# The flag of an exact-path branch summed on TensorE instead of GpSimd, the last projections issued ahead of the branch, and one normalised tile moved later on ScalarE

## The chip, the cores and the metric

The kernel runs on one core of one Trainium2 chip. The time is device microseconds of one execution; the kernel before had a median of 961.63 us over three executions (959.44, 961.63 and 963.8). The profiled execution took 960.48 us by the same clock, and its trace spans 958.4 us from the first to the last instruction.

## The reference

The input x has 2 x 2048 rows of 1024 numbers in float32, here 4096 tokens. What is computed, cut to what matters:

```python
xn = layernorm(x)                              # along the 1024
f = rfft(xn); corr = irfft(f * conj(f))        # autocorrelation of each token
weights, delay = top_k(corr, 6)
p = softmax(weights)
s = sum_k p[k] * roll(xn, -delay[k])
gate = silu(lin(xn, w1q, a1, b1)); up = lin(xn, w3q, a3, b3)
g = silu(lin(gate * up, w2q, a2, b2))          # lin: tiled quarter weight + 0.5 * low-rank part
out = x + s * g
```

Where the autocorrelation at lag 0 stands far above all others, the softmax puts its whole weight on lag 0 and s is xn itself. The kernel proves that for each token by a bound, and has a general path for a group in which a token fails it.

## The kernel before, in words

The 4096 tokens go through in eight groups (i = 0 to 7) of four tiles (q = 0 to 3) of 128 tokens. Each engine has a program of its own, written out in order, and semaphores tie them together. The hidden width is worked through as 22 row blocks of 128 ("pairs", p = 0 to 21; p = 21, LAST, has 64 rows).

**Up stage of group i.** For each p, TensorE makes gate and up products in three rotating pairs of banks (`up`, L1066, with the low-rank part in `lora`, L1083). ScalarE takes silu of the gate (`gate`), VectorE multiplies (`product`, L725, into `h`) and adds four pairs into a chunk (`add_chunk`, L737). Every four pairs TensorE projects `h` on a2 into the bank `zb` (`z2`, L1142). In the same stage the next group is made ready, tile by tile: VectorE's `stats(i + 1, q)` at p = 1, 7, 13, 19; GpSimd's `spread` (L439 to L444, the scale and shift of the normalisation); ScalarE's `normalise` at p = 2, 8, 14, 20 (`xn`); GpSimd's `differences` and `sums` (`ab`, `hl`, which SP's queue transposes into `ft` and `xt`); VectorE's `project` (L680, four per tile; those of tile 3 are `last_projections`).

**The flag.** At p = 5, 9, 11, 15 TensorE computes a part of the power spectrum and the lags from it in the bank `mb` (`odd_power`, `lags`), and VectorE's `lag_gap` takes maxima from it. At p = 16 `lag_gap` writes `rest` (L715): for each of 128 partitions, how many of its four tokens fail the bound. `rest_done` is signalled, and GpSimd adds `rest` over the partitions (L498, `partition_all_reduce`) as the first thing of its turn q = 3, ahead of `spread(i + 1, 3)`; in group 0 five subtractions `w2_low` (L478, 128x1024 each) stand between the two.

**Down stage of group i.** `down` multiplies the folded chunks `hf` by w2 into four token tiles: TensorE's order is chunk 0 of tile 0, `z2` of pairs 16 to 19, chunks 1 and 2, `z2` of pairs 20 and 21 (it waits for `product` of p = 21), chunks 3 and 4, chunks 0 to 4 of tile 1, the tail chunk of both tiles (L1169 ends a tile), tile 2, then `z_across(i + 1)` (four transposes of `zs`, L1128) and tile 3. Meanwhile VectorE and ScalarE finish the tail chunk (`tail_sums`, `folded_low`, in group 0 also `w2_tail`) and `z2_stack`, whose end (`z2_read`) the tail chunk waits for. Then VectorE tests the flag (L1031), loads it into a register (L1033) and branches. In both branches it runs `last_projections(i + 1)` and then, in the one that is taken here, `multiply` and `add_input` for each tile (L859, L864), with `z_split` (L690 to L698, writes `zs`) after tile 0.

ScalarE runs its program in order too: `normalise(i + 1, 3)` at p = 20 stands ahead of `gate(i, 21)`.

Of the kernel before, what the change touches and what calls it, by code (L numbers as in the profile page):

```python
# [8 lines left out]
ACT = mybir.ActivationFunctionType  # L9
ALU = mybir.AluOpType  # L10
AX_X = mybir.AxisListType.X
RADD = bass.bass_isa.ReduceOp.add

P = 128
L = 1024
# [75 lines left out]
def build(nc, d):  # L91
# [3 lines left out]
    with ExitStack() as ctx:  # L95
# [9 lines left out]
        def sem(name):  # L105
            return ctx.enter_context(nc.semaphore(name))
# [65 lines left out]
        zp = [sb(f"zp{k}", [P, 4, 4], BF16) for k in range(3)]  # L172
        rm = sb("rm", [P, 4], F32)
        gp = sb("gp", [P, 4], F32)
        rest = sb("rest", [P, 1], F32)
        rest_all = sb("rest_all", [P, 1], F32)
        some = sb("some", [P, 1], I32)
        raw_a2 = sb("raw_a2", [P, NP_, 2], F32)
        v8 = sb("v8", [P, 8], F32)
# [85 lines left out]
        diff_done, ab_done, sum_done, hl_done = sem("diff_done"), sem("ab_done"), sem("sum_done"), sem("hl_done")  # L265
        z_done, zs_done, zt_ready, zst_done = sem("z_done"), sem("zs_done"), sem("zt_ready"), sem("zst_done")
        c_ready, sq_done, i_ready, gap_done = sem("c_ready"), sem("sq_done"), sem("i_ready"), sem("gap_done")
        rest_done, rall_done = sem("rest_done"), sem("rall_done")
        g_ready, u_ready, sil_done, mult_done = sem("g_ready"), sem("u_ready"), sem("sil_done"), sem("mult_done")
        acc_done, hfh_done, hfl_done = sem("acc_done"), sem("hfh_done"), sem("hfl_done")  # L270
        shift_done, half_done, hft_done, b2h_done = sem("shift_done"), sem("half_done"), sem("hft_done"), sem("b2h_done")
# [11 lines left out]
        def at_group(i, per, n):  # L283
            return i * per + n
# [1 line left out]

        STATS_AT, NORM_AT = (1, 7, 13, 19), (2, 8, 14, 20)
        Z_AT = {3 + 6 * q + r: (q, r) for q in range(3) for r in range(4)}
        C_AT, I_AT = (5, 9), (11, 15)


        def front_buf(i, q):
# [139 lines left out]
        @block.gpsimd  # L432
        def _(pool):
            tt, cp = nc.gpsimd.tensor_tensor, nc.gpsimd.tensor_copy

            def spread(i, q):
                n = i * 4 + q
                pool.wait_ge(stats_done, n + 1)
                tt(ve[:, q:q + 1], mv[:, q, 1:2], three[:, 0:1], ALU.add).then_inc(dev_done, 1)  # L439
                tt(nm[:, q:q + 1], mv[:, q, 0:1], three[:, 2:3], ALU.mult)  # L440
                pool.wait_ge(dev_done, 3 * n + 1)
                tt(rs[:, q:q + 1], ve[:, q:q + 1], three[:, 1:2], ALU.pow).then_inc(dev_done, 1)
                pool.wait_ge(dev_done, 3 * n + 2)
                tt(nm[:, q:q + 1], nm[:, q:q + 1], rs[:, q:q + 1], ALU.mult).then_inc(dev_done, 1)  # L444

            def differences(i, q):
                n, x = i * 4 + q, normal_buf(i, q)
                pool.wait_ge(normed, n + 1)
                if i == 0:
                    pool.wait_ge(hl_done, 2)  # L450
                    if q:
                        pool.wait_ge(ab_done, 3 * n)
                tt(yh[:], x[:, 0:HALF], x[:, HALF:L], ALU.subtract).then_inc(diff_done, 1)
                if n:
                    pool.wait_ge(ft_loaded, 16 * n)
                pool.wait_ge(diff_done, n + 1)
                tt(ab[:, 1:DQ], yh[:, 1:DQ], yh[:, HALF - 1:DQ:-1], ALU.subtract).then_inc(ab_done, 1)
                tt(ab[:, DQ + 1:HALF], yh[:, 1:DQ], yh[:, HALF - 1:DQ:-1], ALU.add).then_inc(ab_done, 1)
                cp(ab[:, 0:DQ + 1:DQ], yh[:, 0:DQ + 1:DQ]).then_inc(ab_done, 1)

            def sums(i, q):
                n, x = i * 4 + q, normal_buf(i, q)
                pool.wait_ge(normed, n + 1)
                if i:
                    pool.wait_ge(ab_done, 3 * n + 3)
                tt(yh[:], x[:, 0:HALF], x[:, HALF:L], ALU.add).then_inc(sum_done, 1)
                pool.wait_ge(sum_done, at_sum(i, q, 1))
                tt(xq[:], yh[:, 0:DQ], yh[:, DQ:HALF], ALU.add).then_inc(sum_done, 1)
                if i and q == 0:
                    pool.wait_ge(xt_loaded, 16 * 4 * i)  # L470
                pool.wait_ge(sum_done, at_sum(i, q, 2))
                cp(hl[:, q, 0:DQ], xq[:]).then_inc(sum_done, 1)
                pool.wait_ge(sum_done, at_sum(i, q, 3))
                tt(hl[:, q, DQ:HALF], xq[:], hl[:, q, 0:DQ], ALU.subtract).then_inc(hl_done, 1)

            def w2_low(n):
                pool.wait_ge(w2h_done, n + 1)
                tt(w2_l[:, n, :], raw_w2[:, n, :], w2_h[:, n, :].bitcast(F32), ALU.subtract).then_inc(w2l_done, 1)  # L478

            for n, value in enumerate((EPS, -0.5, -1.0)):  # L480
                nc.gpsimd.memset(three[:, n:n + 1], value).then_inc(zeroed, 1)
            nc.gpsimd.memset(ones[:], 1.0).then_inc(zeroed, 1)
            pool.wait_ge(zeroed, 4)
            for q in range(4):
                spread(0, q)
            sums(0, 0)
            sums(0, 1)
            nc.gpsimd.memset(zs[:], 0.0).then_inc(zeroed, 1)
            for q in range(4):
                differences(0, q)  # L490
            pool.wait_ge(c_loaded, 16 * 3)
            for u in range(3):
                cp(a2st[:, :, 2 * u:2 * u + 2], raw_a2[:]).then_inc(a2_done, 1)
            for i in range(NG):
                for q in range(4):
                    if q == 3:
                        pool.wait_ge(rest_done, i + 1)
                        nc.gpsimd.partition_all_reduce(rest_all[:], rest[:], P, RADD).then_inc(rall_done, 1)  # L498
                        for n in range(HN if i == 0 else 0):
                            w2_low(n)  # L500
                    if i + 1 < NG:
                        spread(i + 1, q)
                        differences(i + 1, q)
                        sums(i + 1, q)
# [3 lines left out]
        def _(act):  # L508
# [114 lines left out]
            for i in range(NG):  # L623
                last = i + 1 == NG
                for p in range(NP_):
                    gate(i, p)
                    if i == 0 and p in HIGH_AT:
                        w_high(HIGH_AT[p])
                    if i == 0 and p in LOW_AT and LOW_AT[p][1] in (0, 2):
                        b_high(LOW_AT[p][0], LOW_AT[p][1] // 2)  # L630
                    if i == 0 and p in W2_AT:
                        w2_high(W2_AT[p])
                    if p in C_AT:
                        square(i, C_AT.index(p))
                    if not last and p in NORM_AT:
                        normalise(i + 1, NORM_AT.index(p))
                    if p % 4 == 1 and p > 1:
                        folded_high(i, p // 4 - 1)
                    if i == 0 and p == LAST:
                        b2_high()  # L640
                tail_shifts(i)
                folded_high(i, HN)
                z2_copies(i)
                for q in range(4):
                    if not last and q == 3:
                        z_copy(i + 1)
                    down(i, q)
# [3 lines left out]
        def _(dve):  # L651
# [31 lines left out]
            def last_projections(i):  # L683
                for r in range(4):
                    project(i, 3, r)
# [311 lines left out]
            nc.vector.memset(hf_l[64:P, HN, :].bitcast(F32), 0.0)  # L997
            w_tops(2, 6)
            w_scale(2, 6)
            dve.wait_ge(zeroed, 5)  # L1000
            for i in range(NG):
                last = i + 1 == NG
                current(i)
# [23 lines left out]
                if i == 0:  # L1027
                    w2_tail()
                z2_stack(i)
                dve.wait_ge(rall_done, i + 1)  # L1030
                ts(some[:], rest_all[:], 0.0, None, ALU.is_gt)  # L1031
                drain()
                flag = dve.value_load(some[0:1, 0:1])  # L1033
                with dve.If(flag > 0):
                    if not last:
                        last_projections(i + 1)
                        z_split()
                    for q in range(4):
                        general(i, q)
                with dve.Else():  # L1040
                    if not last:
                        last_projections(i + 1)
                    for q in range(4):
                        multiply(i, q)
                        add_input(i, q)
                        if not last and q == 0:
                            z_split()
# [3 lines left out]
        def _(pe):  # L1051
# [60 lines left out]
            def lags(i, k):  # L1112
# [7 lines left out]
                        o = mm(mb[:, DQ * j:DQ * j + DQ], sq[:, c, t], inv[:, 0, :], start=c == 0, stop=c == 1)  # L1120
                o.then_inc(i_ready, 1)

            def z_across(i):
                pe.wait_ge(zs_done, i)
                if i:
                    pe.wait_ge(gap_done, at_group(i - 1, 2, 2))
                for q in range(4):
                    o = nc.tensor.transpose(mb[:, q * P:(q + 1) * P], zs[:, q, :], ident[:])  # L1128
                o.then_inc(zt_ready, 1)
# [52 lines left out]
            for q in range(4):  # L1182
# [3 lines left out]
                for k in range(8):  # L1186
                    o = nc.tensor.transpose(x_banks[k][:, q * P:(q + 1) * P],
                                            normal_buf(0, q)[:, k * P:(k + 1) * P], ident[:])
                    if q == 3:
                        o.then_inc(x_ready, 1)  # L1190
            pe.wait_ge(zeroed, 4)

            def w_tops(first, count):
                pe.wait_ge(wsum_done, first + count)
# [17 lines left out]
            for i in range(NG):  # L1212
                last = i + 1 == NG
                pe.wait_ge(xt_loaded, 16 * 4 * (i + 1))
                for p in range(NP_):
# [8 lines left out]
                        odd_power(i, C_AT.index(p))  # L1224
                    if p in I_AT:
                        lags(i, I_AT.index(p))
                down(i, 0, range(0, 1))
                z2(i, ZB - 2)
                down(i, 0, range(1, 3))
# [55 lines left out]
```

## Time and profile before

| | |
|---|---|
| median of 3 executions | 961.63 us |
| profiled execution, its span | 960.48 us, 958.4 us |
| TensorE busy (matmul) | 868.9 us, 91% of the span |
| VectorE busy | 640.9 us, 67% |
| ScalarE busy | 298.6 us, 31% |
| GpSimd busy | 301.3 us, 31% |
| mean granted clock of TensorE | 0.949 of full speed |

In the rows, PE is TensorE (PEld its weight loads), DVE VectorE, ACT ScalarE, POOL GpSimd, SP the engine that issues the transfers. A row of a timeline is: start, duration (both us), engine, line, operation, out<-in, shape and count; in brackets how long the engine had been idle before it, and what it had waited for. Where several instructions are merged in a row, its duration is from the first to the last. "issue" is idle time for which the profile shows no wait. A row of stretches is: from:to, its length, then the busy time (and count of instructions) of PE, PEld, DVE, ACT and POOL, the granted clock of TensorE as a share of full speed, the busy share of the transfer engines, and GB/s.

### The profile page before, as it was taken

The page shows a single profiled execution, that of the slowest core. Times are in us where ns is not written, and L with a number is a line of the kernel's source. Part 1 is how long each engine was busy: PE and PEld are TensorE (multiplying, and loading weights), DVE is VectorE, ACT ScalarE, POOL GpSimd, SP SyncE. Part 2 cuts the span into 40 slices and gives each one's busy share as a digit, 9 for nine tenths or more (in the row PEclk, how much of TensorE's full clock was granted, in tenths as well). Part 3 has the DMA queues.
Part 4 walks back from the last instruction along what each step waited for, and adds up shares of the span by engine and source line. Part 5 has one row for each costly group of instructions (what it writes and reads, how often), then busy time and mean ns, then how long its engine had stood idle before and what let it go on. Part 6 is the DMA issues. An engine that isn't in the chain of part 4 may idle for free.

```text
span 958.4 us, 11140 instructions
## 1 busy us (share of the span) xinstructions
PE 868.9 (91%) x4034; PEld 444.6 (46%) x4034; DVE 640.9 (67%) x1007; ACT 298.6 (31%) x441; POOL 301.3 (31%) x401
## 2 busy tenths in 40 slices
PE   3868857899899997999979998999979998999997
PEld 3323325644365434843446343844447443653465
DVE  7578834777675795578846786667846776653444
ACT  4653504133222333133232332223322331323221
POOL 6444443034321443034430453133430343300000
PEclk9789977999989997999989999999979999899999
DMA  9735102321034101321124110431023210140003
GB/s 313 202 114 146 28 0 50 111 88 34 28 82 167 34 28 44 116 89 34 28 51 160 38 36 26 124 124 34 28 50 110 89 34 7 43 161 1 1 1 132
DMA packets 53719, 71.53 MB, mean 75 GB/s; under 512 B 37152, under 2 KB 39424, under 8 KB 53392
## 3 DMA queue, kind: packets, MB, share of 16 engines
q1 hardware_dynamic: 53648, 70.69, 23.8%
q8 instruction: 31, 0.51, 0.2%
q14 instruction: 40, 0.33, 0.1%
HBM read 45.51 MB, written 16.78 MB: 65 GB/s over the span
## 4 chain that ended last, share of the span: by engine, by line
PE 58%; DVE 15%; issue 11%; DVEq 7%; SPq 3%; ACT 3%; POOL 3%; DMA 0%; ACTq 0%; POOLq 0%
PE g L1066 14%; PE u L1066 13%; PE zb L1142 4%; PE g L1166 4%; PE u L1166 4%; DVEq L741 4%; DVE junk L680 4%; DVE h L725 4%; PE u L1173 3%; PE g L1173 3%; PE g L1175 3%; PE u L1175 3%; PE g L1083 2%; ACT sil L510 2%; DVE acc L737 1%
## 5 line engine op out<-in xcount | busy, mean ns | idle before, releaser
L1066 PE MATMUL g<-xt,w_h 128*128 128x512 f16 x672 | 203.3, 384 | 10.1 <-DVE w_l L911 5.5
L510 ACT ACTIVATE sil<-g,winv 128x512 f32<-128x512 f32 (+1 forms) x176 | 120.1, 683 | 268.6 <-PE g L1083 224.7
L1066 PE MATMUL u<-xt,w_h 128*128 128x512 f16 x672 | 202.0, 383 | 0.0
L725 DVE SCALAR_TENSOR_TENSOR h<-u,winv,sil 128x512 f32<-128x512 f32 x168 | 125.7, 748 | 97.8 <-ACT sil L510 83.0
L680 DVE CUSTOM_DVE_ANT_0 junk<-xn,abc 128x1024 bf16<-128x1024 f32 x112 | 155.5, 1388 | 32.2 <-issue 28.6
L439 POOL TENSOR_TENSOR ve<-mv,three 128x1 f32<-128x1 f32 x32 | 6.8, 211 | 389.6 <-DVE mv L663 339.4
L1066 PE MATMUL g<-xt,w_l 128*128 128x512 f16 x336 | 128.7, 383 | 0.0
L1066 PE MATMUL u<-xt,w_l 128*128 128x512 f16 x336 | 128.1, 381 | 0.0
L1066 PEld LDWEIGHTS u<-xt,w_h 128*128 128x128 f16 x672 | 66.3, 99 | 81.0 <-issue 3.0
L1066 PEld LDWEIGHTS g<-xt,w_h 128*128 128x128 f16 x672 | 57.2, 98 | 97.7 <-issue 35.9
L1142 PE MATMUL zb<-h,a2st 128*6 128x512 f32 (+1 forms) x352 | 70.2, 639 | 35.5 <-DVE h L725 35.5
L1166 PE MATMUL g<-w_h,hf_h 128*128 128x512 f32 x192 | 83.0, 432 | 9.9 <-POOL w_l L478 9.9
L859 DVE SCALAR_TENSOR_TENSOR ob<-xr,c_mean,gg 128x1024 f32<-128x1024 f32 x32 | 41.0, 1282 | 64.8 <-ACT gg L510 64.0
L1166 PE MATMUL u<-w_h,hf_h 128*128 128x512 f32 x192 | 79.0, 412 | 0.0
L510 ACT ACTIVATE gg<-g 128x512 f32<-128x512 f32 x32 | 19.2, 599 | 172.3 <-PE g L1169 119.0
L510 ACT ACTIVATE xn<-xf,nm,rs 128x1024 f32<-128x1024 f32 x29 | 35.9, 1239 | 102.7 <-POOL nm L444 102.7
L1173 PE MATMUL u<-w_l,hf_h 128*128 128x512 f32 x160 | 66.2, 414 | 0.0
L1173 PE MATMUL g<-w_l,hf_h 128*128 128x512 f32 x160 | 66.1, 413 | 0.0
L1175 PE MATMUL u<-w_h,hf_l 128*128 128x512 f32 x160 | 66.0, 412 | 0.0
L1175 PE MATMUL g<-w_h,hf_l 128*128 128x512 f32 x160 | 65.9, 412 | 0.0
L737 DVE TENSOR_TENSOR acc<-acc,h 128x512 f32<-128x512 f32 x80 | 64.0, 799 | 0.0
L1166 PEld LDWEIGHTS g<-w_h,hf_h 128*128 128x128 f32 x192 | 38.5, 201 | 39.5 <-issue 30.1
(163 smaller groups left out, 1184.7 us busy)
## 6 DMA issues: line engine op xcount, KB each, us to landing
xr<-in_x SPq DMA_DIRECT2D x34, 512.0 KB, 4.7
out_x<-ob SPq DMA_DIRECT2D x32, 512.0 KB, 2.9
xf<-in_x SPq DMA_DIRECT2D x30, 512.0 KB, 3.5
raw_w<-in_w2t SPq DMA_DIRECT2D x1, 2560.0 KB
raw_w<-in_w1t SPq DMA_DIRECT2D x3, 768.0 KB, 7.9
raw_w<-in_w3t SPq DMA_DIRECT2D x3, 768.0 KB, 9.5
abc<-in_a SPq DMA_DIRECT2D x1, 2048.0 KB, 14.0
xt<-hl SPq DMA_TRANSPOSE x32, 3.4
```

The costliest lines, as they stand in the source:

```text
L510: return nc.scalar.activation(out, in_, f, **kw)
L680: nc.vector.tensor_tensor_reduce(junk[:], normal_buf(i, q)[:], abc[:, r, :], 1.0, 0.0, ALU.mult, ALU.add, zt[:, q, r:r + 1]).then_inc(z_do ...
L725: stt(out=h[0:n, p % NH, :], in0=up, scalar=winv[0:n, 2 * (p // 6) + 1:2 * (p // 6) + 2], in1=sil[0:n, p % 2, :], op0=ALU.mult, op1=ALU.mu ...
L737: o = tt(acc[0:rows, b, :], a, h[0:rows, p % NH, :], ALU.add)
L741: drain()
L859: stt(out=o[:], in0=x[:], scalar=c_mean[:, q:q + 1], in1=gg[:], op0=ALU.subtract, op1=ALU.mult)
L1066: o = mm(bank[:], a, x, start=opens and t == 0, stop=closes and t == len(terms) - 1)
L1083: o = mm((gb, ub)[s % 2][k % 3][:], bst[32 * s:32 * s + 32, p // 2, :], zst[32 * s:32 * s + 32, :], start=s >= 2, stop=s < 2)
L1142: o = mm(zb[c:c + 6, :], a2st[0:rows, p, :], h[0:rows, p % NH, :], start=n == 0, stop=p + 4 >= NP_)
L1166: mm(bank[:], hf_h[:, n, t], w2_h[:, n, c:c + 512], start=n == 0, stop=False)
L1173: mm(bank[:], hf_h[:, n, t], w2_l[:, n, c:c + 512], start=False, stop=False)
L1175: mm(bank[:], hf_l[:, n, t], w2_h[:, n, c:c + 512], start=False, stop=False)
```

## The change

The sum of `rest` over the partitions goes from GpSimd to TensorE: `rest` becomes bfloat16, and one matmul of a 128x128 block of ones (`ones_h`) with it (`flag_sum`, one column, into the first column of `mb`) stands in TensorE's program behind `up(i, 18)`. VectorE's test reads `mb` instead of `rest_all`, and signals `flag_read`, for which `z_across` now waits before it overwrites `mb`. `last_projections(i + 1)` moves from both branches to ahead of the test. On ScalarE, `normalise(1, 3)`, in group 0 alone, moves from p = 20 to behind `z2_copies(0)`.

```diff
-        rest = sb("rest", [P, 1], F32)
-        rest_all = sb("rest_all", [P, 1], F32)
+        rest = sb("rest", [P, 1], BF16)
+        ones_h = sb("ones_h", [P, P], BF16)
...
-        C_AT, I_AT = (5, 9), (11, 15)
+        C_AT, I_AT, FLAG_AT = (5, 9), (11, 15), 18
...
             nc.gpsimd.memset(ones[:], 1.0).then_inc(zeroed, 1)
-            pool.wait_ge(zeroed, 4)
+            nc.gpsimd.memset(ones_h[:], 1.0).then_inc(zeroed, 1)
+            pool.wait_ge(zeroed, 5)
...
                     if q == 3:
-                        pool.wait_ge(rest_done, i + 1)
-                        nc.gpsimd.partition_all_reduce(rest_all[:], rest[:], P, RADD).then_inc(rall_done, 1)
                         for n in range(HN if i == 0 else 0):
                             w2_low(n)
...
-                    if not last and p in NORM_AT:
+                    if not last and p in NORM_AT[:3 if i == 0 else 4]:
                         normalise(i + 1, NORM_AT.index(p))
...
                 z2_copies(i)
+                if i == 0:
+                    normalise(1, 3)
...
                 z2_stack(i)
+                if not last:
+                    last_projections(i + 1)
                 dve.wait_ge(rall_done, i + 1)
-                ts(some[:], rest_all[:], 0.0, None, ALU.is_gt)
+                ts(some[:], mb[:, 0:1], 0.0, None, ALU.is_gt).then_inc(flag_read, 1)
                 drain()
                 flag = dve.value_load(some[0:1, 0:1])
                 with dve.If(flag > 0):
                     if not last:
-                        last_projections(i + 1)
                         z_split()
                     for q in range(4):
                         general(i, q)
                 with dve.Else():
-                    if not last:
-                        last_projections(i + 1)
                     for q in range(4):
...
+            def flag_sum(i):
+                pe.wait_ge(rest_done, i + 1)
+                mm(mb[:, 0:1], ones_h[:], rest[:], start=True, stop=True).then_inc(rall_done, 1)
+
             def z_across(i):
                 pe.wait_ge(zs_done, i)
-                if i:
-                    pe.wait_ge(gap_done, at_group(i - 1, 2, 2))
+                pe.wait_ge(flag_read, i)
...
                     if p in I_AT:
                         lags(i, I_AT.index(p))
+                    if p == FLAG_AT:
+                        flag_sum(i)
```

## Rows read from the trace of the kernel before

**Rows 1.** Waits of TensorE, 187 to 960 us: engine, line, releaser, us, times, longest.

```profile
PE zb L1142 <- DVE h L725: 30.4, 6, 5.6
```

**Rows 2.** Busy time in stretches: one up stage, six down stages (summed), the last one.

```profile
187.40:254.10 66.70, 66.70 (x347) 27.02 (x347) 54.51 (x84) 22.22 (x32) 27.97 (x37) 1.00 0.17 54
259.48:296.96 37.48, 32.91 (x127) 23.61 (x127) 21.43 (x34) 10.35 (x17) 8.86 (x12) 0.91 0.34 103
...
811.36:849.89 38.53, 32.91 (x126) 23.62 (x126) 21.43 (x34) 10.34 (x17) 8.85 (x12) 0.91 0.27 86
sum 230.18, PE 199.82 PEld 143.46 DVE 128.74 ACT 62.05 POOL 53.12; mean PE 33.30 PEld 23.91 DVE 21.46 ACT 10.34 POOL 8.85
921.87:951.41 29.54, 29.54 (x123) 22.29 (x122) 9.98 (x10) 5.20 (x10) 0.00 (x0) 1.00 0.25 90
```

**Rows 3.** Timelines of VectorE and GpSimd around the reduction of group 1.

```profile
246.42 0.15 DVE L715 TENSOR_SCALAR rest<-gp 128x1 f32<-128x1 f32 x1
246.13 0.67 POOL L474 TENSOR_TENSOR hl<-xq,hl 128x256 f16<-128x256 f32 x1
252.98 0.40 POOL L498 PARTITION_ALL_REDUCE rest_all<-rest  x1 [6.18 <-issue]
260.21 0.18 POOL L439 TENSOR_TENSOR ve<-mv,three 128x1 f32<-128x1 f32 x1 [6.83 <-issue]
```

**Rows 4.** Timelines of the other engines, from group 1's last statistics to TensorE.

```profile
254.42 0.21 DVE L663 BATCH_NORM_AGGREGATE mv<-bn 128x2 f32<-128x12 f32 x1
261.40 1.24 ACT L510 ACTIVATE xn<-xf,nm,rs 128x1024 f32<-128x1024 f32 x1 [7.97 <-POOL nm L444]
263.24 0.75 DVE L725 SCALAR_TENSOR_TENSOR h<-g,winv,sil 64x512 f32<-64x512 f32 x1 [7.35 <-ACT sil L510]
264.05 3.67 PE L1142 MATMUL zb<-h,a2st 128*6 128x512 f32 x4 [4.57 <-DVE h L725]
```

**Rows 5.** Timelines of VectorE and TensorE, from the flag to the transposes, groups 1 and 3.

```profile
272.86 0.15 DVE L1031 TENSOR_SCALAR some<-rest_all 128x1 int32<-128x1 f32 x1
276.82 1.23 DVE L680 CUSTOM_DVE_ANT_0 junk<-xn,abc 128x1024 bf16<-128x1024 f32 x1 [3.80 <-issue]
285.75 0.71 DVE L698 CAST zs<-zp 128x64 f32<-128x64 bf16 x6
288.58 0.60 PE L1128 MATMUL mb<-ident,zs 128*128 128x128 f32 x4
...
499.39 1.23 DVE L680 CUSTOM_DVE_ANT_0 junk<-xn,abc 128x1024 bf16<-128x1024 f32 x1 [4.69 <-issue]
508.32 0.70 DVE L698 CAST zs<-zp 128x64 f32<-128x64 bf16 x6
```

**Rows 6.** Timelines of group 0: VectorE's flag input, GpSimd, TensorE, VectorE.

```profile
120.40 0.15 DVE L715 TENSOR_SCALAR rest<-gp 128x1 f32<-128x1 f32 x1
133.31 11.63 POOL L478 TENSOR_TENSOR w_l<-raw_w,w_h 128x1024 fp32r<-128x1024 f32 x5 [7.01 <-issue]
147.94 0.75 DVE L725 SCALAR_TENSOR_TENSOR h<-g,winv,sil 64x512 f32<-64x512 f32 x1 [18.06 <-ACT sil L510]
177.45 0.66 PE L1128 MATMUL mb<-ident,zs 128*128 128x128 f32 x4 [2.81 <-DVE zs L698]
187.43 0.61 PE L1066 MATMUL g<-xt,w_h 128*128 128x512 f16 x2
```

**Rows 7.** Timelines of GpSimd and VectorE, one collision; the 0.68 us row undisturbed.

```profile
222.96 1.27 POOL L466 TENSOR_TENSOR yh<-xn 128x512 f32<-128x512 f32 x1
223.03 1.75 DVE L737 TENSOR_TENSOR acc<-h 128x512 f32<-128x512 f32 x1
227.83 0.68 DVE L737 TENSOR_TENSOR acc<-acc,h 128x512 f32<-128x512 f32 x1
```

**Rows 8.** TensorE at p = 19, where `flag_sum` is put, and `rest`: group 3.

```profile
467.38 0.39 PE L1083 MATMUL g<-zst,bst 32*128 32x512 bf16 x1
467.72 0.15 DVE L715 TENSOR_SCALAR rest<-gp 128x1 f32<-128x1 f32 x1
```

More of the change, by code:

```diff
@@ L11 @@
 AX_X = mybir.AxisListType.X
-RADD = bass.bass_isa.ReduceOp.add
 P = 128
@@ L267, in build @@
         c_ready, sq_done, i_ready, gap_done = sem("c_ready"), sem("sq_done"), sem("i_ready"), sem("gap_done")
-        rest_done, rall_done = sem("rest_done"), sem("rall_done")
+        rest_done, rall_done, flag_read = sem("rest_done"), sem("rall_done"), sem("flag_read")
         g_ready, u_ready, sil_done, mult_done = sem("g_ready"), sem("u_ready"), sem("sil_done"), sem("mult_done")
@@ L999, in _ @@
             w_scale(2, 6)
-            dve.wait_ge(zeroed, 5)
+            dve.wait_ge(zeroed, 6)
             for i in range(NG):
@@ L1190, in _ @@
                         o.then_inc(x_ready, 1)
-            pe.wait_ge(zeroed, 4)
+            pe.wait_ge(zeroed, 5)
             def w_tops(first, count):
```

## The prediction, made before the changed kernel was seen

> **What bounds the kernel now.** The page's busy shares come first: TensorE has 91% of the span, so the question is where its other 9% lies. The waits of TensorE from group 1 on have one entry, 30.4 us in six times: the last `z2` of a group waits for `product` of p = 21 [rows 1]. The stretches show the rest. In an up stage TensorE is busy for all of its 66.70 us at full clock [rows 2]. The six down stages of groups 1 to 6, each from the moment when that wait begins to the first matmul of the next group, take 230.18 us together [rows 2]; that of group 7, which has no such wait and keeps the full clock, takes 29.54 us [rows 2]. The granted clock of the six is 0.91 or so, that is, a part of each ran at 1.2 GHz instead of 2.4: TensorE had idled for 4.57 us before, and its first four matmuls afterwards take 3.67 us [rows 4]. So the wait costs its own length and then a slow stretch.
>
> Why is `product` late? It waits for the gate's silu, which stands behind `normalise(i + 1, 3)` on ScalarE, which waits for the scale from GpSimd [rows 4]. The statistics are there at 254.42 + 0.21 = 254.63, but GpSimd takes them up at 260.21, because the reduction is in its way: `rest` is there at 246.57, GpSimd is free at 246.80, and yet the 0.40 us reduction starts after 6.18 us of idling and is followed by 6.83 us more [rows 3]. The reduction takes 13.4 us of GpSimd, and 5.5 us of that end on the path.
>
> **The change, part by part.** *The reduction leaves GpSimd.* `spread(i + 1, 3)` then follows the statistics as elsewhere, about 0.08 us behind: 254.71 instead of 260.21, 5.50 us earlier. By the same reading it is 5.5 to 5.9 us in groups 2 to 6. `product` of p = 21 follows, 263.24 - 5.50 = 257.74, and is read 0.81 us after its start [rows 4], at 258.55. TensorE gets there at 264.05 - 4.57 = 259.48 [rows 4]. The wait is gone, with 0.9 us to spare (0.2 in the tightest, group 6), and with it what took the clock down. The down stage should then be group 7's 29.54 us plus the transposes of `zs`, which group 7 lacks, 0.44 us at full clock from the start of one to the next matmul (my estimate from their 0.60 us row [rows 5]): 29.98. Six of them are 179.9 us, so 230.2 - 179.9 = 50.3 us are to be had.
>
> *What is late next.* The transposes wait for `zs`. VectorE's chain (tail chunk, `z2_stack`, projections, flag, tile 0, split) has no idle time that waits for TensorE in group 1, so it moves by the same 5.50 us: `zs` is written at 285.75 + 0.71 - 5.50 = 280.96 [rows 5]. TensorE moves by more: it gets there at 288.6 to 288.7 now [rows 5], and 37.48 - 29.98 = 7.5 us earlier then, about 281.1. No wait, but only just. In group 3 the stretch from the flag to the first projection was about 1 us longer (4.69 us idle against 3.80 [rows 5]), `zs` comes at 508.32 + 0.70 - 5.88 = 503.14, and TensorE, at 480.15 + 21.6, stands 1.4 us. The other four are within 0.3 us. I take 1.4 us off.
>
> *The matmul on TensorE.* One weight load and one column. Its price is not in the trace; the up stage's load-and-matmul pairs come every 0.2 us with 512 columns, so it lies between nothing and 0.3 us; 0.1 a group, nearer to an empty pass, 0.8 us in all (group 0 hides it). Its wait is more serious: behind `flag_sum` stands `up(i, 19)`, that is, all of TensorE. In group 3 `rest` is ready at 467.87, and TensorE would be there at 467.38 [rows 8]: 0.5 us. By the same two rows it is nothing in groups 1, 2, 4 and 7 (0.1 us either way), 0.3 in 5 and 0.6 in 6. In group 3 it is swallowed by the wait for `zs`; 0.9 us stay. In group 0 it is 3.1 us (`rest` ends at 120.55 [rows 6]), covered: VectorE, not TensorE, is behind there, and TensorE then idles for the subtractions.
>
> *Projections ahead of the flag.* The same instructions in another order on VectorE, with `multiply` now right behind the branch. Nothing waits between. 0. If the branch hid a part of its 3.8 us behind them now, it would be a gain of up to that; the test stands behind them in order, so it can't. `z_across`'s new wait for `flag_read` is met long before `zs_done`: 0.
>
> *Group 0.* Without the reduction `w2_low` starts at 120.1 instead of 133.31 [rows 6], and `gate(0, 21)` no longer waits for the tile's normalisation. That would put `product` of p = 21 at 129.9 instead of 147.94 [rows 6], if VectorE kept its pace. It will not. The subtractions now run beside VectorE's `add_chunk`, projections and `folded_low`, all with two SBUF inputs, where before VectorE idled beside them (18.06 us [rows 6]). One collision: a GpSimd operation runs from 222.96 to 224.23, and an addition of VectorE's that starts at 223.03 takes 1.75 us against 0.68 undisturbed: it ends 0.55 us after GpSimd's does [rows 7]. So it was held for GpSimd's whole operation. Five subtractions of 2.33 us, one VectorE operation let in between each two: `product` of p = 21 comes at about 139.0, 8.9 us earlier than before. From there VectorE's tail goes as before, but `normalise(1, 3)` now comes after `z2_copies` and holds the projections back by 0.45 us, and GpSimd's work on that tile now collides with the projections: 2.4 us by the same reckoning. 8.9 - 0.45 - 2.4 leaves 6 us for `zs`, and for the transposes (177.45 before) and the next group (187.43 before [rows 6]), which follow it. Bounds: 17 us if nothing is held, 4 us if GpSimd always goes first. The Trainium skill, in "SBUF — State Buffer" (section SBUF: two separate sides), says that the port pair the two engines share is an exclusive lock which one operation holds to its end. By that rule, the trace agrees; shared bandwidth instead would give group 0 some 12 us.
>
> The sum: 50.3 - 1.4 - 0.9 - 0.8 + 6 = 53.2 us off the profiled 960.48, 907.3. The median of before is 1.15 us above its profiled execution, so about 908.5.
>
> **Rivals.** *The transposes become the bound everywhere.* For: the margins at `zs` are 0.0 to 0.3 us, and group 0 shows what follows a 2.81 us idling there, a slow stretch of 9.98 us to the next group [rows 6] where 34 matmuls at full rate take 7.9. Against: the chain moves as a whole and the fall of the clock was seen only after 2.8 us or more of idling. Price: 1 us of waiting and 2.1 of slow clock in each of six groups, 19 us: 927.
>
> *Group 0 keeps its gain.* If subtractions and VectorE get along, 17 instead of 6: 897.5. Against it, rows 7.
>
> *Slower: the flag holds TensorE.* `up(i, 19)` waits for `rest` in every group. It decides when `rest` comes more than 50.3 / 7, about 7.2 us, behind `up(i, 18)`; seen are 3.1 us once and at most 0.6 otherwise. If `rest` were 8 us late, with 2 us of slow clock: 7 x 10 = 70 against 50, some 980. The Trainium skill's "GPSIMD Engine Reference" (section 4.1 Engine selection) gives reductions along partitions to GpSimd, and by it the move would be a loss; here the 13.4 us of rows 3 speak against that.
>
> *The change does nothing:* the idle time around the reduction is something else's and stays. Against: it stands on both sides of the reduction [rows 3], and in group 0 as well, where a subtraction follows after 7.01 us [rows 6]. 960.
>
> **How the numbers follow.** Forecast 0.60, group 0's large gain 0.13, transposes 0.19, nothing 0.04, slower 0.04. What a measurement of this kernel can tell from no change is 0.5%, 4.8 us. The forecast's own range is 903 to 914 (0 to 0.3 us for the matmul, group 0 from 4 to about 10). The range reaches down into the large gain, to 898, and up into the transposes' case, to 921. Faster 0.93, same 0.03, slower 0.04.
>
> **What would show it.** Right: GpSimd starts `ve` of tile 3 within 0.2 us of `mv`; no wait of `zb` for `h` from group 1 on; PEclk 1.00 through the down stages; these near 30 us; `w2_low` from 120 on and stretched over 15 us; `product` of p = 21 near 139. Wrong: waits of TensorE on `rest`, or on `zs` of more than 1 us in most groups with a low clock behind them; up stages longer than 66.7 us, since nothing here says that the earlier work of GpSimd disturbs them.

## The result, and the profile after

The changed kernel takes 904.56 us (median of four executions, 903.65 to 904.94) against 960.9 us of the kernel before (median of four, one more than in the table above): a ratio of 0.9409, 95% interval 0.9385 to 0.9433. The forecast was 908.5 in 898 to 921. The profiled execution took 903.65 us against 960.48, its trace spans 901.9 us against 958.4.

Two parts of the page of the changed kernel, busy time and granted clock (in this kernel L1124 is `flag_sum`, L1144 `z2`, L1130 `z_across`, L1168 `down`, L1033 the test of the flag, L438 `spread`, L477 `w2_low`, L508 ScalarE):

```profile
PE 848.8 (94%) x4042; PEld 437.6 (49%) x4042; DVE 649.8 (72%) x1007; ACT 299.1 (33%) x441; POOL 304.6 (34%) x394
...
PEclk9898988899999999999999999999999999999999
```

Waits of TensorE in it from 187 us on, all of them:

```profile
PE mb L1124 <- DVE rest L715: 0.2, 1, 0.2
```

The 30.4 us of [rows 1] are gone and nothing has come in their place. Stretches of the changed kernel: the up stage of group 1, the first and the last of the six down stages with the sum of the six, and group 7's:

```profile
180.98:252.99 72.01, 72.01 (x373) 30.15 (x373) 57.84 (x90) 25.61 (x37) 30.70 (x42) 1.00 0.16 50
...
252.99:282.97 29.98, 29.98 (x128) 22.69 (x127) 19.86 (x32) 6.95 (x13) 5.83 (x7) 1.00 0.47 128
...
763.38:793.37 29.99, 29.99 (x128) 22.69 (x127) 19.86 (x32) 6.95 (x13) 5.83 (x7) 1.00 0.36 110
sum 179.92, PE 179.92 PEld 136.15 DVE 119.20 ACT 41.69 POOL 34.97; mean PE 29.99 PEld 22.69 DVE 19.87 ACT 6.95 POOL 5.83
...
861.38:890.92 29.54, 29.54 (x127) 21.58 (x127) 12.75 (x15) 7.56 (x14) 0.00 (x0) 1.00 0.21 72
```

The down stages fell from 230.18 to 179.92 us [rows 2], 8.4 us a group, with TensorE busy all the time at full clock. Group 0 is read below.

Timelines of group 1 of the changed kernel (GpSimd, VectorE, ScalarE, TensorE), which answer to [rows 3 to 5]:

```profile
247.97 0.21 DVE L663 BATCH_NORM_AGGREGATE mv<-bn 128x2 f32<-128x12 f32 x1
248.26 0.19 POOL L438 TENSOR_TENSOR ve<-mv,three 128x1 f32<-128x1 f32 x1 [7.91 <-DVE mv L663]
249.53 1.24 ACT L508 ACTIVATE xn<-xf,nm,rs 128x1024 f32<-128x1024 f32 x1 [2.52 <-POOL nm L443]
251.38 0.75 DVE L725 SCALAR_TENSOR_TENSOR h<-g,winv,sil 64x512 f32<-64x512 f32 x1 [1.93 <-ACT sil L508]
252.99 1.97 PE L1144 MATMUL zb<-h,a2st 128*6 128x512 f32 x4
...
265.99 0.15 DVE L1033 TENSOR_SCALAR some<-mb 128x1 int32<-128x1 f32 x1
269.59 1.28 DVE L859 SCALAR_TENSOR_TENSOR ob<-xr,c_mean,gg 128x1024 f32<-128x1024 f32 x1 [3.45 <-issue]
273.58 0.70 DVE L698 CAST zs<-zp 128x64 f32<-128x64 bf16 x6
274.60 0.60 PE L1130 MATMUL mb<-ident,zs 128*128 128x128 f32 x4
```

GpSimd takes the statistics up 0.08 us after they are there (248.18), instead of 5.58 us. `product` of p = 21 is written by 252.1, TensorE comes for it at 252.99, and its matmuls take 1.97 us instead of 3.67. `zs` is there at 274.28; TensorE comes 0.3 us later.

The flag's pass on TensorE, in groups 1 and 4 of the changed kernel, with VectorE's `rest`:

```profile
239.97 0.16 DVE L715 TENSOR_SCALAR rest<-gp 128x1 bf16<-128x1 f32 x1
240.18 0.18 PE L1124 MATMUL mb<-rest,ones_h 128*128 128x1 bf16 x1
...
546.57 0.18 PE L1124 MATMUL mb<-rest,ones_h 128*128 128x1 bf16 x1 [0.22 <-DVE rest L715]
```

In group 1 it is free: from the start of the up stage to the last `z2` it is 72.01 us with the pass and 72.05 without it (187.43 to 259.48 before). Only in group 4 is `rest` late, by 0.22 us.

Group 0 of the changed kernel, VectorE, GpSimd and TensorE, beside [rows 6]:

```profile
122.19 0.16 DVE L715 TENSOR_SCALAR rest<-gp 128x1 bf16<-128x1 f32 x1
121.73 14.45 POOL L477 TENSOR_TENSOR w_l<-raw_w,w_h 128x1024 fp32r<-128x1024 f32 x5
128.04 3.17 DVE L680 CUSTOM_DVE_ANT_0 junk<-xn,abc 128x1024 bf16<-128x1024 f32 x1
131.15 2.81 DVE L758 TENSOR_TENSOR hf_l<-acc,hf_h 128x512 fp32r<-128x512 f32 x1
139.74 0.75 DVE L725 SCALAR_TENSOR_TENSOR h<-g,winv,sil 64x512 f32<-64x512 f32 x1
134.68 0.80 PE L1168 MATMUL g<-w_h,hf_h 128*128 128x512 f32 x1 [3.07 <-DVE h L725]
170.77 1.12 PE L1130 MATMUL mb<-ident,zs 128*128 128x128 f32 x4 [5.88 <-DVE zs L698]
180.98 0.60 PE L1065 MATMUL g<-xt,w_h 128*128 128x512 f16 x2
```

The projection takes 3.17 us beside the subtractions (1.22 undisturbed), `folded_low` 2.81 (0.68 undisturbed), and TensorE stands 3.07 us for a `product` that is held behind them. The transposes come 5.88 us after TensorE is ready for them. What the span lost, by stage: up to `rest` of group 0 it is 1.80 us longer (120.55, 122.35); from there to group 1's first matmul it fell from 66.88 to 58.63, 8.25 us; groups 1 to 6 from 662.46 (187.43 to 849.89) to 612.39 (180.98 to 793.37), 50.07 us; the rest is the same. Together 56.5 us, the difference of the spans. The first of these is within what executions differ by: in the nine other profiled executions below that have no edit ahead of that point but the changed kernel's own (all but the one with memsets), `rest` of group 0 came at 120.6 to 124.3 us. The second differs too: in the two other traces of the changed kernel it takes 59.61 and 58.18 us instead of 58.63, so group 0's gain from `rest` on is 7.3 to 8.7 us against the one trace of before.

### The profile page after: what moved, and what is told of

It reads as the page before. It is cut to its first block, busy times and chain, and to the rows that moved or that the text cites. A ratio compares the mean times of both kernels' runs of the same rounds, so it can differ in the third digit from the quotient of the medians.

```text
span 901.9 us, 11119 instructions
## 1 busy us (share of the span) xinstructions
PE 848.8 (94%) x4042; PEld 437.6 (49%) x4042; DVE 649.8 (72%) x1007; ACT 299.1 (33%) x441; POOL 304.6 (34%) x394
## 4 chain that ended last, share of the span: by engine, by line
PE 79%; DVE 11%; ACT 3%; DVEq 3%; issue 3%; POOL 0%; DMA 0%; SPq 0%; ACTq 0%
PE g L1065 22%; PE u L1065 20%; PE zb L1144 5%; PE g L1168 5%; PE u L1168 5%; PE u L1177 4%; PE u L1175 4%; PE g L1177 4%; PE g L1175 4%; PE g L1082 3%; DVE junk L680 2%; DVEq L741 2%; DVE h L725 1%; DVE acc L737 1%; ACT w_abs L508 1%
## 5 line engine op out<-in xcount | busy, mean ns | idle before, releaser
L508 ACT ACTIVATE sil<-g,winv 128x512 f32<-128x512 f32 (+1 forms) x176 | 120.0, 683 | 280.2 <-PE g L1082 237.6
L680 DVE CUSTOM_DVE_ANT_0 junk<-xn,abc 128x1024 bf16<-128x1024 f32 x112 | 160.1, 1430 | 6.4 <-issue 2.2
L438 POOL TENSOR_TENSOR ve<-mv,three 128x1 f32<-128x1 f32 x32 | 6.8, 212 | 366.8 <-DVE mv L663 366.8
L1168 PE MATMUL g<-w_h,hf_h 128*128 128x512 f32 x192 | 80.5, 419 | 3.1 <-DVE h L725 3.1
L1168 PE MATMUL u<-w_h,hf_h 128*128 128x512 f32 x192 | 77.0, 401 | 0.0
L508 ACT ACTIVATE gg<-g 128x512 f32<-128x512 f32 x32 | 19.1, 598 | 158.8 <-PE g L1171 87.1
L1177 PE MATMUL u<-w_h,hf_l 128*128 128x512 f32 x160 | 64.0, 400 | 0.0
L1175 PE MATMUL u<-w_l,hf_h 128*128 128x512 f32 x160 | 64.0, 400 | 0.0
L1175 PE MATMUL g<-w_l,hf_h 128*128 128x512 f32 x160 | 63.5, 397 | 0.0
L1177 PE MATMUL g<-w_h,hf_l 128*128 128x512 f32 x160 | 63.5, 397 | 0.0
L1144 PE MATMUL zb<-h,a2st 128*6 128x512 f32 (+1 forms) x352 | 58.4, 603 | 0.0
L452 POOL TENSOR_TENSOR yh<-xn 128x512 f32<-128x512 f32 x29 | 39.0, 1344 | 56.2 <-ACT xn L508 56.2
L1065 PEld LDWEIGHTS g<-xt,w_l 128*128 128x128 f16 x336 | 33.2, 99 | 40.9 <-issue 2.1
```

What stands on the lines that cost most here:

```text
L508: return nc.scalar.activation(out, in_, f, **kw)
L680: nc.vector.tensor_tensor_reduce(junk[:], normal_buf(i, q)[:], abc[:, r, :], 1.0, 0.0, ALU.mult, ALU.add, zt[:, q, r:r + 1]).then_inc(z_do ...
L1065: o = mm(bank[:], a, x, start=opens and t == 0, stop=closes and t == len(terms) - 1)
L1144: o = mm(zb[c:c + 6, :], a2st[0:rows, p, :], h[0:rows, p % NH, :], start=n == 0, stop=p + 4 >= NP_)
L1168: mm(bank[:], hf_h[:, n, t], w2_h[:, n, c:c + 512], start=n == 0, stop=False)
L1175: mm(bank[:], hf_h[:, n, t], w2_l[:, n, c:c + 512], start=False, stop=False)
```

## The experiments

The first four ran beside each other, with the kernel before at 957.8 us. What was expected of each stands ahead of its result.

**The sum on TensorE alone** (the other two edits undone):

```diff
-                    if not last and p in NORM_AT[:3 if i == 0 else 4]:
+                    if not last and p in NORM_AT:
...
-                if i == 0:
-                    normalise(1, 3)
...
-                if not last:
-                    last_projections(i + 1)
                 dve.wait_ge(rall_done, i + 1)
...
                 with dve.If(flag > 0):
                     if not last:
+                        last_projections(i + 1)
                         z_split()
...
                 with dve.Else():
+                    if not last:
+                        last_projections(i + 1)
```

> Only the sum of the flag moves to TensorE; the projections stay in the branches and the tile's normalisation stays at p = 20. If the reduction's 13.4 us on GpSimd were the cause, the wait of the last z2 for h is gone from groups 1 to 6 and the six down stages fall from 230.2 us to 180 plus what the transposes wait: with the projections behind the branch (3.77 to 4.85 us from flag to first projection in the kernel before, 3.5 to 3.7 from flag to multiply in the changed one) VectorE's zs comes 0.2 to 1.2 us later against a margin of 0.3 to 0.8, so 0 to 1 us a group: 904 to 910. Rival (the order on VectorE carries part of the gain): over 912.

905.88 us, 0.946 of the kernel before (0.9439 to 0.9481). Of the 54.8 us that the changed kernel gained beside it, 51.9 are the reduction's leaving GpSimd alone, as the prediction had it.

**The changed kernel with the projections back in the branches** (the last two hunks above):

> The changed kernel with the last projections back in both branches. My prediction gave their place nothing: 904 to 905. With the margin at the transposes of 0.3 us and a branch some 0.2 to 1.2 us dearer ahead of them: 0 to 1 us a group, 904 to 910, with waits of the transposes for zs in the trace. Rival: the branch hides behind queued projections in the changed kernel, then multiply comes 1 us or more later here in every group and the time is over 908.

906.2 us, 0.9464 (0.9441 to 0.9487). The changed kernel itself, once more:

> The changed kernel once more beside the others: 903.5 to 905.5. It also shows whether rest of group 0, which came 1.8 us later (122.35 against 120.55 us), is late in every execution of it (then the change causes it) or moves between executions.

902.97 us, 0.9433 (0.9414 to 0.9451). The intervals overlap, but the traces tell them apart: groups 1 to 6 take 615.92 us (179.59 to 795.51) with the projections in the branches, 615.75 in the kernel with the sum alone, and 612.39, 612.28 and 612.67 in three executions of the changed kernel. So the place of the projections is worth some 3.4 us, where I had given it nothing. Timelines of VectorE and TensorE, groups 1 and 3, projections in the branch:

```profile
259.65 0.16 DVE L1031 TENSOR_SCALAR some<-mb 128x1 int32<-128x1 f32 x1
265.05 1.23 DVE L680 CUSTOM_DVE_ANT_0 junk<-xn,abc 128x1024 bf16<-128x1024 f32 x1 [5.24 <-issue]
273.98 0.70 DVE L698 CAST zs<-zp 128x64 f32<-128x64 bf16 x6
...
470.02 1.23 DVE L680 CUSTOM_DVE_ANT_0 junk<-xn,abc 128x1024 bf16<-128x1024 f32 x1 [4.63 <-issue]
...
274.74 0.65 PE L1131 MATMUL mb<-ident,zs 128*128 128x128 f32 x4 [1.37 <-DVE zs L698]
```

And its waits of TensorE from 185 us on:

```profile
PE mb L1131 <- DVE zs L698: 2.1, 2, 1.4
PE mb L1125 <- DVE rest L715: 0.8, 2, 0.6
```

From the flag to the first instruction behind the branch it is 5.40 us in group 1 and 4.79 in group 3, 3.7 to 3.85 in the others. The kernel with the sum alone shows 5.35 and 4.79 in the same two groups, the kernel before 4.85 in group 3 [rows 5]. With the projections ahead of the flag it was 3.48 to 4.06 in all 21 branches of three executions. The late `zs` stops TensorE for 2.1 us, `rest` for 0.8 instead of 0.2, and 0.8 us of the 3.5 I can't place (0.7 of it lies in the three down stages of groups 1, 3 and 5, 0.2 each beyond the wait, at full clock). Group 3 is slow in all four kernels that have the projections in the branch (4.6 us in the one with the reduction later, below), group 1 in two of them, the others in none; the data are the same in every kernel, and with the projections ahead of the flag no group is slow. That speaks against the data as the cause. Where the instructions lie is my guess, which nothing here tests; the Trainium skill says, in "Runtime: NRT & Kernel Launch" (section Instruction fetch mechanics), that a taken branch to a target outside the instructions held has to fetch it first. That would fit, but no run here shows the fetch.

**The changed kernel with the tile's normalisation at p = 20** (the first two hunks above):

> The changed kernel with the normalisation of tile (1, 3) back at p = 20, ahead of the last gate of group 0. The statistics of that tile come at 138.4 us there and product of p = 21 at 139.7, so the gate waits about 2 us for it; the projections no longer wait 0.4 us and GpSimd's work on the tile collides with the tail instead of with the projections. Groups 1 to 7 are the same. By my reckoning -1 to +2 us: 903.5 to 906.5. Rival (this move matters, several us of group 0 come from it): over 907.

903.52 us, 0.9443 (0.9424 to 0.9462): no difference from 902.97 that can be told. From `rest` of group 0 to group 1 it is 57.63 us here, and 58.63, 59.61 and 58.18 in the changed kernel. The traces show two things that cancel. With the tile at p = 20, `product` of p = 21 comes 19.31 us after `rest` instead of 17.39, and `zs` 0.6 to 0.8 us later. But TensorE then waits for `zs` only 1.14 us instead of 5.9 to 6.0, and from the transposes to group 1 it then has the full clock:

```profile
170.04:178.48 8.44, 8.44 (x39) 6.71 (x39) 5.00 (x4) 1.57 (x3) 0.00 (x0) 1.00 0.67 246
```

The same stretch takes 10.21, 11.03 and 9.75 us in the three traces of the changed kernel, at a granted clock of 0.81, 0.74 and 0.85. So this edit brings nothing; what the earlier `product` gains, the slow clock takes back, and most of the 1.4 us by which the three differ comes from that clock.

Four more ran beside the kernel before at 959.94 us. **The reduction kept on GpSimd, one place later** (an edit of the kernel before alone):

```diff
                     if q == 3:
-                        pool.wait_ge(rest_done, i + 1)
-                        nc.gpsimd.partition_all_reduce(rest_all[:], rest[:], P, RADD).then_inc(rall_done, 1)
                         for n in range(HN if i == 0 else 0):
                             w2_low(n)
                     if i + 1 < NG:
                         spread(i + 1, q)
+                    if q == 3:
+                        pool.wait_ge(rest_done, i + 1)
+                        nc.gpsimd.partition_all_reduce(rest_all[:], rest[:], P, RADD).then_inc(rall_done, 1)
+                    if i + 1 < NG:
                         differences(i + 1, q)
```

> The kernel before with one edit: the reduction stays on GpSimd, but behind spread(i + 1, 3) instead of ahead of it (in group 0 behind the five subtractions). If its place ahead of the scale was the trouble and not its engine, the wait of the last z2 for h is gone as in the changed kernel. The differences of the tile come 13.4 us later, though (about 269 instead of 257 in group 1), so GpSimd collides with the projections in the branch, worth up to 2.4 us a group at the transposes, and the tile's transposes into xt land near 282, close to the next group's start: 50 us less 2 to 4 us in each of six groups, 920 to 932. Rival (GpSimd must be free of the reduction): no gain over 15 us, 943 or more. Rival (TensorE as its engine added nothing): 903 to 908.

917.88 us, 0.9554 (0.953 to 0.9578): 42 of some 57 us, from the order on GpSimd alone. It is 2 us under the range that I had given. Its GpSimd in group 1 and its waits of TensorE:

```profile
248.45 0.31 POOL L444 TENSOR_TENSOR nm<-nm,rs 128x1 f32<-128x1 f32 x1
254.58 0.40 POOL L503 PARTITION_ALL_REDUCE rest_all<-rest  x1 [5.82 <-issue]
261.74 1.28 POOL L453 TENSOR_TENSOR yh<-xn 128x512 f32<-128x512 f32 x1 [6.76 <-issue]
```

```profile
PE mb L1130 <- DVE zs L700: 10.8, 6, 2.3
```

The idle time goes wherever the reduction goes: 5.82 us ahead of it, 6.76 behind. The wait of `z2` is gone, but GpSimd's work on the tile now runs into the projections and the tiles behind them, and TensorE waits 10.8 us in six times for `zs`. In group 1 three of the four projections take 1.91, 1.63 and 1.63 us instead of 1.23. Groups 1 to 6 take 628.55 us, 16.2 more than in the changed kernel.

**The subtractions of group 0 replaced by memsets** in the changed kernel; the low part of w2 is left out:

```diff
-                tt(w2_l[:, n, :], raw_w2[:, n, :], w2_h[:, n, :].bitcast(F32), ALU.subtract).then_inc(w2l_done, 1)
+                nc.gpsimd.memset(w2_l[:, n, :].bitcast(F32), 0.0).then_inc(w2l_done, 1)
```

> The changed kernel with the five subtractions w2_low of group 0 replaced by five memsets of the same tiles, so the low part of w2 is left out: GpSimd writes the same bytes and reads nothing. If the subtractions hold VectorE's two-input operations for their whole length, product of p = 21 comes about 8 us sooner after rest (17.4 us in the changed kernel, 9.4 if nothing holds) and the first matmul of group 1 some 7 us sooner after rest (58.6 there). If the two engines share, both stay within 2 us. Groups 1 to 7 are the same; one time near 896 against near 903.

One execution, 897.46 us. Timelines of it, VectorE, GpSimd and TensorE:

```profile
120.98 1.87 DVE L711 TENSOR_SCALAR rm<-gp 128x4 f32<-128x4 f32 x1
123.16 0.16 DVE L715 TENSOR_SCALAR rest<-gp 128x1 bf16<-128x1 f32 x1
123.97 1.22 DVE L680 CUSTOM_DVE_ANT_0 junk<-xn,abc 128x1024 bf16<-128x1024 f32 x1
120.99 4.54 POOL L477 MEMSET w_l<- 128x1024 f32 x5
133.70 0.75 DVE L725 SCALAR_TENSOR_TENSOR h<-g,winv,sil 64x512 f32<-64x512 f32 x1
174.92 0.60 PE L1065 MATMUL g<-xt,w_h 128*128 128x512 f16 x2
```

From `rest` to `product` of p = 21 it is 10.38 us instead of 17.39, to group 1 51.60 instead of 58.63. The subtractions hold VectorE for 7 us behind `rest`, and all of it reaches group 1. The memsets are shorter (4.54 us in all against 14.45) and read nothing. That one projection ran wholly beside them in its undisturbed 1.22 us speaks for the reading and not the length, but one row is little. And they are not harmless: `rm` (L711), 0.17 us in the changed kernel, starts with the first of them and takes 1.87 us, so `rest` itself is 1.7 us late here. Counted from the row ahead of `rm` (120.73 here, 121.45 in the changed kernel) the gain to group 1 is 5.3 us and not 7.0.

**The flag one pair sooner** (`FLAG_AT` 17 instead of 18) in the changed kernel:

> The changed kernel with flag_sum one pair sooner, behind up(i, 17). It prices the wait in TensorE's queue: rest comes 2.6 us after TensorE gets there in each of groups 1 to 6, as the flag's place at 18 leaves nothing to spare and an up pair takes 2.6 us. If TensorE sets the pace, each of these is paid in full, 6 x 2.6 = 16 us, and group 7 too if rest is late there: 918 to 922, more if the clock falls behind each wait. Rival (VectorE's tail sets the pace at the transposes and hides it): under 908.

928.57 us, 0.9678 (0.9648 to 0.9707). Its waits of TensorE from 185 us on, and the stretch behind the wait in group 1:

```profile
PE mb L1124 <- DVE rest L715: 16.0, 7, 2.9
```

```profile
240.10:257.20 17.10, 17.00 (x76) 7.91 (x76) 11.21 (x19) 5.66 (x8) 3.88 (x8) 0.90 0.00 0
```

Six of the waits are 2.4 to 2.9 us, paid in full (the seventh, in group 7, is 0.4), and behind five of them the granted clock falls to half for a while (0.90 over these 17 us); behind the sixth, 2.44 us in group 3, it does not (1.00 over the 15.5 us that follow). Groups 1 to 6 take 635.45 us, 23.1 more than the changed kernel, of which 15.6 is waiting. The time is 6.6 us over the range that I had given. The waits are as I had reckoned; the slow clock behind them, named but not in the number, makes up the rest.

**Another order in group 0** of the changed kernel. TensorE waited 5.9 us there for `zs`. Tiles 0 and 1 are finished ahead of the projections, and the transposes come behind tile 3:

```diff
-                if not last:
+                if i and not last:
                     last_projections(i + 1)
...
                     if not last:
+                        if i == 0:
+                            last_projections(i + 1)
                         z_split()
...
                         add_input(i, q)
-                        if not last and q == 0:
+                        if i == 0 and q == 1:
+                            last_projections(i + 1)
+                        if not last and q == (0 if i else 1):
                             z_split()
...
-                if not last:
+                if i and not last:
                     z_across(i + 1)
                 down(i, 3, range(0, HN + 1))
+                if i == 0:
+                    z_across(i + 1)
```

> The changed kernel with another order in group 0 alone: the flag is tested before the last projections, tiles 0 and 1 are multiplied and added first, then the projections and the split follow; on TensorE the four transposes of zs come behind tile 3 instead of ahead of it. TensorE waits 5.9 to 6.0 us for zs in group 0 of the changed kernel, at the low clock behind it. If that wait is real cost, group 1 starts 6 to 8 us sooner: 895 to 898. Rival: tile 3 waits for tile 1's read instead, or the next group for tile 2's, and it stays within 2 us of 903.

896.43 us (895.22 to 897.04), 0.9336 (0.9317 to 0.9354). TensorE in its group 0:

```profile
171.40 0.66 PE L1134 MATMUL mb<-ident,zs 128*128 128x128 f32 x4 [0.29 <-DVE zs L698]
171.90 0.59 PE L1069 MATMUL g<-xt,w_h 128*128 128x512 f16 x2
```

From `rest` (120.62) to group 1 it is 51.28 us instead of 58.63: the wait is 0.29 us instead of 5.88, and the down stage of group 0 has a granted clock of 1.00 instead of 0.91.

**With the flag one pair later as well** (`FLAG_AT` 19), beside the changed kernel, the kernel before at 959.46 us:

> The kernel with the new order in group 0 (tiles 0 and 1 ahead of the last projections, transposes behind tile 3), and flag_sum one pair later as well, behind up(i, 19). TensorE waited 0.7 us for rest in groups 1 to 7 with it at 18 and 3.1 us in group 0, where it is hidden. A pair later rest has been there for 2 us or more: no such wait, 0.7 us less, 894 to 896.5, and 0.991 to 0.993 of the changed kernel beside it. If the wait at 18 cost nothing, the same 896.4 as before.

> The changed kernel in the same rounds, for a direct comparison: 902.5 to 905.

895.83 us (894.08 to 896.47), 0.9332 (0.9315 to 0.9349), against 902.32 us, 0.9411 (0.9395 to 0.9427). This version beats the kernel before and the changed kernel, both measured beside it. No wait for `rest` is left in its trace from 165 us on, and groups 1 to 6 take 612.14 us there against 612.91 with the flag at 18; in the times (0.9332 against 0.9336) so small a gain can't be told.

## Why the prediction was right, point by point

In the traces the forecast had 53.2 us and 56.5 came. Groups 1 to 6 were to give 47.2 (50.3 less 1.4, 0.9 and 0.8) and gave 50.07. Group 0 was to give 6 and gave 8.25 from `rest` on, but the stretch ahead of `rest` happened to be 1.80 us longer in this execution. That the second miss hardly shows in the total is luck.

- *The reduction leaves GpSimd, 50.3 us.* Groups 1 to 6 gained 50.07, the down stages alone 50.26. The scale follows the statistics at 0.08 us, each down stage takes 29.98 or 29.99 us where 29.98 was forecast. The kernel with the sum alone shows the cause, and the one with the reduction later shows that the idle time is the reduction's own and that being ahead of the scale was what cost.
- *1.4 us for a late `zs` in group 3:* it did not come. The term took the slow branch of group 3 as given and the projections' new place as worth nothing, and both were one thing: with the projections ahead of the flag no branch of the three executions took over 4.06 us. With them inside, group 3 and, worse, group 1 are late. This is the step that failed: the place of the projections, put at nothing, is worth 3.4 us; with its 0, the forecast described the experiment with the projections in the branches better than the changed kernel.
- *0.9 us of waiting for `rest`, 0.8 us for the pass:* 0.22 us of waiting in one group. The pass costs nothing that shows. Counted from its group's first matmul, `rest` comes 0.4 and 0.7 us later than usual in groups 5 and 6 of the kernel before and again with the projections in the branches (waits of 0.24 and 0.57 us there), and 0.4 us later in group 4 in all three executions of the changed kernel. So in these groups it goes with the program and not with the data; group 3, 0.6 us late in the trace of before, differs between executions of one kernel (0.3 us in one of the three, nothing in the others). In group 6 the trace of before shows where it comes from: `rm`, 0.17 us elsewhere, takes 0.56 and ends with an operation of GpSimd's, behind 0.42 us of idling instead of 0.09.

```profile
798.15 0.56 DVE L711 TENSOR_SCALAR rm<-gp 128x4 f32<-128x4 f32 x1 [0.42 <-issue]
798.02 0.67 POOL L474 TENSOR_TENSOR hl<-xq,hl 128x256 f16<-128x256 f32 x1
```

  In the changed kernel the two no longer meet there. For the other groups the cause is open.
- *Group 0, 6 us:* 8.25 from `rest` on. From `rest` to `product` of p = 21 I had 18.4 us, it took 17.4; the projections were drawn out from 4.96 to 6.74 us, 1.8 where I had 2.4. The memset experiment gives 7.0 us to the hold behind `rest`, of the 9.1 reckoned. The Trainium skill's exclusive lock ("SBUF — State Buffer", section SBUF: two separate sides) agrees with this trace: single operations of VectorE are held for up to 2.1 us, about one subtraction (2.36 us alone), and the subtractions, 2.79 to 3.33 us beside them, are held in their turn.
- *The flag holds TensorE*, the slower rival, did not come, but is nearer than I had it. I put its deciding point at `rest` 7.2 us late; with it 2.5 us late the kernel is some 24 us slower (23.6 by the spans). The kernel before paid 8.4 us a group for waits of 4.5 to 5.6, so I estimate that some 5 us would be enough. At p = 18 there is almost nothing to spare.
- *The transposes as the bound:* they are not that in the changed kernel; `zs` is there 0.2 to 0.4 us before TensorE comes, where the forecast had 0.0 to 0.3. That small margin is what makes the projections' place worth anything. The kernel with the reduction later is this rival come true, with waits of 1.3 to 2.3 us in all six groups and 16.2 us more than the changed kernel. My price of 2.1 us for each slow stretch was too high: it was 1.55 (9.98 against 8.43), and in three groups only.
- The move of the normalisation was folded into group 0's term. Alone it is worth nothing that shows in the time.

## What to carry to other kernels

A small instruction can cost its engine far more than its own time: look at the idle time on both sides of it, and at what stands behind it in the queue. Moving the 0.40 us reduction behind one short step gave three quarters of the gain, with no other engine taking it over. When a wait is taken off an engine that sets the pace, the slow clock behind the wait is a part of the price, here 3 to 4 us on top of 5; read it from a stage of the same work that has no wait.

## What the runs showed of the hardware that was not expected

- The reduction over partitions on GpSimd, 0.40 us in its row, keeps the engine some 13 us: 5.7 to 6.4 us idle ahead and 6.6 to 7.6 behind, in either place. In the trace of before, two instructions of GpSimd's sequencer stand ahead of the first idle time (group 1):

```profile
L498 POOLq MODIFY_POOL_CONFIG  x2: 11/11/11, 247.0 to 247.0; - x2
```

  Two more, at 253.34 and 253.37 (L439), stand between the reduction and the second idle time. It is so in groups 0 to 6, in either place of the reduction; the traces without it have two such instructions in all, at their start. That the idle time is the work that they ask for is my reading and not shown. The Trainium skill's "GPSIMD Engine Reference" (section 4.1 Engine selection) names GpSimd for it; for this one column, TensorE's pass of 0.18 us was the better: 902 to 906 us against 917.88 with the reduction in the better of its two places.
- A shorter wait than I had thought can cost the clock. With the reduction later, waits of 1.26, 1.61 and 1.75 us of TensorE were followed by 8.4 us to the next group at full clock, and waits of 1.92, 1.99 and 2.31 by 9.98 to 9.99 us, with the clock lowered for a part of it (0.83 over the stretch). With the flag at 17, waits of 2.54 to 2.93 us were followed by a lowered clock, and one of 2.44 was not. I had counted on nothing under 2.8 us; the length of the wait alone doesn't decide it, and these rows give no limit.
- From the flag to the first instruction behind the branch, 3.5 to 5.4 us, it mattered whether the projections lie there: without them it was 4.06 us at most in every trace; with them it was 4.6 to 4.9 us in group 3 of all four such kernels, and 5.4 in group 1 of two.
